# Where SyncE's queue issues the next input's load and the routing record in the first layer's loop with tiles

## The reference, cut to what matters

```python
xn = layernorm(x); s = L0_attn(xn)          # 16 heads of 64, linear attention with elu+1
g = silu(L0_ffn(xn))                        # rmsnorm, causal attention, rmsnorm, top-2 of 8 experts
x = x + s * g
xn = layernorm(x); s = L1_attn(xn)          # chunked gated linear attention, gelu MLP
g = silu(L1_ffn(xn))                        # top-1 of 8 experts
x = x + s * g

def L0_ffn(x):                              # the part the change lies in
    x2 = x + causal_attention(rmsnorm(x))
    h2 = rmsnorm(x2)
    w, e = top2(softmax(h2 @ gate_w.T))     # routing: which experts, which weights
    return x2 + sum_k w[k] * (silu(h2 @ w1[e[k]].T) * (h2 @ w3[e[k]].T)) @ w2[e[k]].T
```

## Time and profile before

| what | value |
|---|---|
| median of 3 runs | 1948.61 us |
| lowest, highest | 1946.26, 1956.49 us |
| the profiled execution's own time | 1937.43 us |
| its span in the profile | 1935.4 us |
| TensorE busy | 1674.1 us, 86% of the span |
| VectorE, ScalarE, GpSimd busy | 64%, 52%, 13% |
| mean granted TensorE clock | 0.96 of full speed |

### The profile page before, as it was taken

One profiled execution on the slowest core, in us unless ns is written; L12 is line 12 of the kernel. 1 busy time (PEld: TensorE's weight loads), 2 busy tenths in 40 slices (PEclk: granted clock), 3 DMA queues, 4 the chain that ended last, 5 costly groups with the idle time before them and its releaser, 6 DMA issues.

```text
span 1935.4 us, 65540 instructions
## 1 busy us (share of the span) xinstructions
PE 1674.1 (86%) x25348; PEld 1273.5 (66%) x25364; DVE 1238.5 (64%) x3535; ACT 1009.3 (52%) x2322; POOL 253.9 (13%) x271
## 2 busy tenths in 40 slices
PE   5999999979888898958998898897889889988866
PEld 3777776757666776745676676765577666676656
DVE  5677677756556666646676766765666666676535
ACT  3555555544555555524655566553544455544445
POOL 0000110000000000030111011101121112110063
PEclk9999999999999999979999999998999999999978
DMA  4333334431222211331222122210222111221244
GB/s 164 135 145 144 155 152 174 187 122 42 62 68 68 79 45 56 102 104 43 78 68 68 59 81 80 62 36 25 64 68 61 43 52 53 68 63 55 75 143 120
DMA packets 97379, 167.82 MB, mean 87 GB/s; under 512 B 15145, under 2 KB 65593, under 8 KB 93882
## 3 DMA queue, kind: packets, MB, share of 16 engines
q1 hardware_dynamic: 87322, 141.59, 21.8%
q0 software_dynamic: 9888, 23.71, 4.1%
HBM read 86.42 MB, written 78.80 MB: 85 GB/s over the span
## 4 chain that ended last, share of the span: by engine, by line
PE 52%; DVE 17%; issue 11%; ACT 11%; SPq 4%; DMA 2%; DVEq 1%; POOL 1%; POOLq 0%; ACTq 0%
PE psum L1007 5%; PE psum L851 4%; PE psum L885 3%; PE psum L997 3%; PE psum L1309 3%; PE psum L1199 3%; PE psum L1297 2%; PE psum L896 2%; PE psum L1045 2%; PE psum L932 2%; PE psum L1224 2%; PE psum L1093 2%; PE psum L936 2%; PE psum L1128 2%; ACT pts L1553 2%
## 5 line engine op out<-in xcount | busy, mean ns | idle before, releaser
L1553 ACT ACTIVATE pts<-psum 128x512 f32<-128x512 f32 x192 | 99.2, 604 | 162.1 <-PE psum L1045 161.4
L725 POOL DMA_INDIRECT rows<-h,recA x64 | 62.2, 972 | 780.7 <-DVE recA L1795 662.9
L1007 PE MATMUL psum<-wall,xT_s 128*128 128x512 f32 x256 | 130.3, 656 | 0.1
L749 POOL DMA_INDIRECT rows<-xn,recC x32 | 36.6, 1143 | 667.1 <-DVE recC L2249 612.9
L885 PE MATMUL psum<-txT,wall 128*128 128x128 f32 x864 | 117.0, 279 | 1.9 <-issue 1.5
L1158 PE MATMUL psum<-xT_s,wall 128*128 128x256 f32 x512 | 115.7, 379 | 0.0
L885 PEld LDWEIGHTS psum<-txT,wall 128*128 128x128 f32 x864 | 109.4, 197 | 4.5 <-issue 2.0
L896 PE MATMUL psum<-wall,tg 128*128 128x128 f32 (+1 forms) x720 | 109.2, 287 | 2.6 <-DVE tg L1743 1.9
L2058 DVE TENSOR_REDUCE mneg<-psum 128x2 f32<-128x512 f32 x128 | 79.4, 684 | 40.2 <-PE psum L1025 39.2
L1158 PEld LDWEIGHTS psum<-xT_s,wall 128*128 128x128 f32 x512 | 96.1, 190 | 13.2 <-issue 0.8
L896 PEld LDWEIGHTS psum<-wall,tg 128*128 128x128 f32 x720 | 94.8, 199 | 7.5 <-DVE tg L1743 5.2
(11 more groups left out here) (273 smaller groups left out, 4237.5 us busy)
## 6 DMA issues: line engine op xcount, KB each, us to landing
wall<-in_wB SPq DMA_DIRECT2D x84, 384.0 KB, 3.0
outs<-pbd SPq DMA_DIRECT2D x16, 1024.0 KB, 7.5
mixed_rows<-pbd SPq DMA_DIRECT2D x16, 899.5 KB, 9.6
wall<-in_wD SPq DMA_DIRECT2D x24, 578.0 KB, 3.7
tx<-rows SPq DMA_DIRECT2D x132, 64.0 KB, 2.8
rows<-pbd SPq DMA_DIRECT2D x64, 128.0 KB, 1.7
rows<-pbd SPq DMA_DIRECT2D x8, 1024.0 KB, 3.9
outs<-ty SPq DMA_DIRECT2D x108, 64.0 KB, 1.6
```

What stands on the lines that cost most here:

```text
L725: nc.gpsimd.indirect_dma_start(rows, bass.IndirectOffsetOnAxis(ap=slotsA[:, c:c + 1], axis=0), h2[:, t, :], None).then_inc(sem("scattered" ...
L1007: mm(bank(f"{name}{t}{c}"), xnT[:, t * P:(t + 1) * P], wqkv0[:, off + c * 512:off + (c + 1) * 512], start=True, stop=True).then_inc(*fills ...
L1553: af(pT[:, n, :], bank(f"e{n}"), ACT.Exp, scale=float(HD) ** -0.5).then_inc(*frees(f"e{n}"))
```

## The change

Only SyncE's program changes. In segment 3, x's load for the next iteration is issued by `record_A`, ahead of the record; `record_A` runs ahead of tile 4 instead of tile 2 (this also in segment 4, which has tiles but no x to load). The first x of segment 3 is loaded after segment 2's loop, ahead of `first_loads`. The last iteration of segment 3 stands behind the loop in a copy of its own, without a load of x.

```diff
-            def body():
+            def body(last=False):
                 stages = now["stages"]
-                if "H" in stages and now["n"]:
+                if now["n"] in (1, 2):
                     sp.wait_ge(*given("x_free", 0))
                     sp.dma_start(x[:, :, :], A["x"][row("H")].rearrange("(t p) d -> p t d", p=P)).then_inc(sem("x_ready"), 16)
...
+                def next_x():
+
+                    sp.wait_ge(*given("x_free"))
+                    sp.dma_start(x[:, :, :], A["x"][row("H") + 1].rearrange("(t p) d -> p t d", p=P)).then_inc(sem("x_ready"), 16)
+
                 def record_A():
+                    if "H" in stages and "B" in stages and not last:
+                        next_x()
                     if "G" in stages:
                         sp.wait_ge(*given("slots_ready"))
                         sp.dma_start(KA[row("G")], recA[:, :]).then_inc(sem("recA_stored"), 16)
...
-                record, place = (record_C, 4) if "C" in stages else (record_A, 2)
+                record, place = (record_C, 4) if "C" in stages else (record_A, 4)
...
                 n = now["n"]
                 if n == 2:
+                    sp.wait_ge(*all_given("x_free"))
+                    sp.dma_start(x[:, :, :], A["x"][rows_before("H") + HB].rearrange("(t p) d -> p t d", p=P)).then_inc(sem("x_ready"), 16)
                     sp.wait_ge(sem("later_zeros"), 16 * (6 + 6 * HB))
                     sp.sem_inc(sem("zeroed"), 1)
...
                 if times == 1:
                     segment(n, 0)
                     body()
+                elif n == 3:
+                    with sp.Fori(0, times - 1) as i:
+                        segment(n, i)
+                        body()
+                    segment(n, times - 1)
+                    body(last=True)
                 else:
```

## The result

Over 6 executions of each, the kernel with the change took 1940.03 us (1937.96 to 1942.29) and the kernel before 1951.96 us (1946.26 to 1957.56): ratio 0.9937, 95% interval [0.9923, 0.9952]. That is 12 us less, where 46.3 were forecast; the time lies 25 us above the range's upper end. The profiled execution of the changed kernel took 1940.23 us with a span of 1938.2 us.

What follows compares the result with a forecast made beforehand. Taken as bound: PE idle and slowed in segment 3, waiting for h2 behind x's late load. 34.6 us of idle and 11.7 us of lower clock make 46.3 us; 1948.6 - 46.3 = 1902.3 us, range 1888 to 1915.

Steps and rivals of the forecast that it cites:

- What bounds the kernel: Segment 3, head of the iterations: DVE waits 39.1 us for x, so PE waits 34.6 us for h2.
- Why x is late: SP's single queue in segment 3: x is issued behind the record and tiles 2 to 5, which take 15.8 us.
- part 6: SP's stores and loads of tiles 2 to 5 go some 6 to 8 us earlier; they bring and cost nothing.
- Parts 1 and 2: Iterations 2 to 6, head: early x ends DVE's wait, nothing else is late, and PE's stage takes 5.79 us.
- Part 3: First iteration of segment 3: x's first load ahead of the first tiles cuts the stage from 17.49 to 5.79 us.
- Part 4: Six stages at the iterations' heads: 81.05 - 6 x 5.79 = 46.3 us gained, bounds 41.9 to 49.9.
- The clock term: PE's products at the iterations' heads: 11.7 us lost to the lower clock come back, bounds 7.3 to 15.3.
- Part 5: Record moved from ahead of tile 2 to ahead of tile 4: issued 1.5 us later, 5.4 us to spare, cost nothing.
- The rivals: Other outcomes: clock stays low, 1914.0 us (0.04); half, 1925.4 (0.02); no change, 1948.6 (0.02); slower, 1960 (0.02).
- a new wait takes half of it: Ahead of h2, the record's or scatter's landing becomes last, sharing DMA engines with two tile loads: 1925.4 us, chance 0.02.
- The mark of failure set down at the end: Prediction fails if segment 3's periods shrink and the time behind segment 3 grows by as much.
- the sign of being right: Segment 3: six periods of about 53 us in place of 59 to 61.

Runs made afterwards that it cites:

- g1: The kernel before, unchanged, profiled again for its trace: 1948.72 us, ratio 0.9999.
- e3: The changed kernel with only x's first load early: next x behind tile 5's load and record ahead of tile 2, as before; 1936.76 us, ratio 0.9938.
- f4: The changed kernel with POOL's scatter in segments 3 and 4 waiting for ScalarE's signal for the second weighted sum's inverse: 1895.58 us, ratio 0.9725.
- e1: The kernel before with only the record moved, from ahead of tile 2 to ahead of tile 4: 1946.84 us, ratio 1.0003.
- h1: The changed kernel with SP waiting behind the record until the scatter has landed, in segments 3 and 4: 1928.21 us, ratio 0.9880.
- g2: The kernel before with POOL's scatter in segments 3 and 4 waiting for ScalarE's signal for the second weighted sum: 1948.91 us, ratio 0.9989.
- g3: The kernel before with x's first load early and POOL's scatter waiting for ScalarE's signal for the second weighted sum: 1930.57 us, ratio 0.9891.
- h2: As a run, not the buffer: the changed kernel with the record back ahead of tile 2 and POOL's scatter waiting for ScalarE's signal: 1901.56 us, ratio 0.9753.
- f3: The changed kernel with 72 of the 96 products with the values left out of the weighted sums in segment 3's loop: 1911.03 us, ratio 0.9789.
- f2: The changed kernel with POOL raising a semaphore nobody reads 150 times in every iteration of segment 3: 1939.18 us, ratio 0.9939.

## Why the prediction was wrong

The stretches at the head and at the end of the six iterations, summed, as measured in each trace:

| kernel | head | end | both | median us |
|---|---|---|---|---|
| before, the execution profiled at first | 81.05 | 32.17 | 113.2 | 1937.43 (one) |
| before, profiled again | 45.86 | 73.43 | 119.3 | 1948.72 |
| changed | 34.29 | 74.08 | 108.4 | 1940.03 |
| before, with POOL's wait | 83.13 | 32.20 | 115.3 | 1948.91 |
| changed, with POOL's wait | 34.80 | 32.20 | 67.0 | 1895.58 |

- **What bounds the kernel, and "Why x is late"**: failed, and everything rests on it. The rows were read rightly, but they were rows of one execution that was not like the others. In the kernel before as g1 shows it, DVE waits 1.8 us in sum for x in iterations 2 to 6, and what sets the period there is the late signal (5.06 to 5.11 us in each), which the prediction had nowhere. It set it in the changed kernel too (59.5 to 61 us). The warning stood in the prediction itself, the median "11 us above it", and was explained away in the same sentence behind part 6: "the gain is a difference of waits that each execution has". It was not.
- **Parts 1 and 2** (x on time, what is late next at the head): right. The stages are 5.80 us where 5.79 was forecast, and there is no wait for x, for the scatter or for h2. DVE's extra work in them costs nothing.
- **Part 3** (x's first load): right in its mechanism, and the only part that shows in the time. It was priced 17.49 - 5.79 = 11.7 us. e3, which has this alone, is at 0.9938 [0.9915, 0.9960], some 12 us, and the change as a whole is too.
- **Part 4** (the sum of 46.3 us): the head gave 46.8 us against the trace it was taken from. Against the kernel as it usually runs, the head gave 45.86 - 34.29 = 11.6 us, and the end took 0.7. The clock term was right in kind: all windows at the head are at 1.00 (in g1 those of iterations 2 to 6 already were). The cited rule of the Trainium skill, page "TensorE: Matmul & The Clock Gate", Part 1, would have dropped it. The trace bears out its figure of under 1% of a span: the slow products in the stretches at the end (6.98 us of PE's busy time each, against 4.80 in f4) make about 13 us in six iterations, 0.7% of 1938. But for a change that was to bring 2.4%, 0.7% is too much to leave out.
- **Part 5** (the record costs nothing): right within what can be told. e1 is at 1.0003 [0.9991, 1.0016].
- **Part 6** ("they bring and cost nothing"): right in the measured time; in e1 the tiles' earlier loads changed nothing. What I did not ask is what the transfers and SP's work around the scatter do to other engines' signals. h1 shows 1.5 us per iteration for tile 4's store and load.
- **The rivals**: none had a delay that the profiled execution did not show. The nearest, "a new wait takes half of it", named the right place (scatter and tile loads at one time) and the wrong victim. The mark of failure set down at the end (periods shrink and the time behind segment 3 grows by as much) is not what was seen either; what failed is the sign of being right ahead of it, periods of about 53 us, which stayed at 59.5 to 61.

In short, two delays lay in parallel. Either one hides the other. Taking away the late signal alone gives nothing (g2: 0.9989), and so does moving x in the loop alone (the changed kernel's 0.9937 is e3's 0.9938). With x's first load early, the signal on time may bring a little (g3, 0.9891, beside e3; the intervals overlap). Taking away both, and the first iteration's wait with them, gives 55.8 us, of which the windows show 119.3 - 67.0 = 52.3. Most of the rest is in segment 4, where the same sum takes 6.77 us in the changed kernel (825.59 to 832.36) and 3.71 in f4 (785.16 to 788.87).

## What to carry to other kernels

Compare the profiled execution's time with the median of the others before building on its waits; when it lies outside their spread, profile the same kernel again, since it may show another bound. When a removed wait gives nothing, look for a second delay of the same size in the same loop, by comparing stretches of two traces that should be alike (here two sums of six windows), and test both removals together. A signal that must get through while POOL starts a scatter can be late: let POOL's start wait for it, if the scatter has time to spare.

## What was unexpected of the hardware

- The signal of a finished product reached ScalarE 5.04 to 5.24 us late in iterations 2 to 6 of every kernel in which PE ended 0.6 us behind the start of POOL's first scatter instruction, except in the first profile of before (and 2.9 to 3.7 us in h1). There PE ended 0.63 us behind it, and ScalarE started 0.07 us later:

```profile
600.09 0.28 ACT L1557 ACTIVATE aden<-psum 128x128 f32<-128x128 f32 x1 [2.83 <-PE psum L1079]
```

- With PE ending 1.57 us ahead of it (f4, g2, g3, h2) or 0.8 us (f3), the signal was on time. In f4 later signals of PE fell inside the scatter and passed (3.69 us for the products for q), and in f3 nothing beyond the low clock shows in them. What decides which signal is held stays open, and so does why the first execution had no late signal.
- In segment 4 it was PE itself that was slowed within the scatter. The last part of the sum in the changed kernel, where 32 products took 1.06 us in f4, and in the first profile of before too (at 832.05, with the scatter starting at 831.61):

```profile
828.23 1.29 PE L1094 MATMUL psum<-pts,ones 128*32 128x128 f32 x21
829.88 0.43 PE L1094 MATMUL psum<-pts,ones 128*32 128x128 f32 x5 [0.36 <-issue]
830.63 0.43 PE L1094 MATMUL psum<-pts,ones 128*32 128x128 f32 x4 [0.32 <-issue]
831.35 0.27 PE L1094 MATMUL psum<-pts,ones 128*32 128x128 f32 x1 [0.29 <-issue]
832.06 0.29 PE L1094 MATMUL psum<-pts,ones 128*32 128x128 f32 x1 [0.44 <-issue]
```

- POOL's instruction takes 0.84 us for 16 rows and 0.96 for 128. Where the signal is late POOL is not held itself. In the loop of the four kernels with the added wait the third of the four instructions takes 1.36 us each time (f4, 578.86); what holds it was not tried. The Trainium skill, page "SBUF — State Buffer", section "SBUF: two separate sides", tells of the opposite case: POOL cannot write its descriptors while certain DVE operations run. The changed kernel's trace shows another thing: POOL's four instructions start every 1.26 us, and DVE is idle from 589.01 to 594.73.
- Whether recording has a part in it is open. Between 110 and 410 us the first trace of before holds 1530 semaphore updates of engines where its instructions make 1529; that kernel profiled again holds 1465 of 1530, the changed one 1449 of 1528. The first trace of before is the only one of the fifteen in which none is missing there, and the only one in which the signal is on time although PE ends behind POOL's start. The Trainium skill, page "NOTIFIC — the notification-queue block", section 7.1, says that the block that writes such records pushes back inside rather than lose one, and that this could slow an engine. No run here shows it. f2's 150 further updates per iteration cost nothing, and f4 is on time with as many records missing (1444 of 1528). Every time in this document is that of an execution whose clock and span were recorded, so executions without any record were not tried.
